# Cross attention and mixture of experts over 64 batches: the last part with fused small steps, a 65/12 split of the keys and new queue orders

## The chip, the cores and the metric

The kernel runs on one core of one Trainium2 chip. The metric is the device time of one execution in microseconds, taken over several runs. Profiles come from one further execution under the hardware profiler. TensorE does the matrix products, VectorE and ScalarE the elementwise work and reductions, GpSimd small side steps, and SyncE starts the transfers.

## What is computed

The reference is four layers, each an attention and a feed-forward part, on x of shape (64, 128, 128), with a context of 77 keys for each batch. Only the fourth layer's code changes. Cut to what matters, for each batch, with features the layer norm of x:

```python
txt_proj = textual_features @ Ws                      # 77 x 128
feat_proj = features @ W                              # 128 x 128
h = tanh(txt_proj[None, :, :] + feat_proj[:, None, :] + b)   # 128 tokens x 77 keys x 128
rho = h @ w + mask                                    # 128 x 77
att = softmax(rho)
txt_h = att @ textual_features
w_s, b_s = tanh(txt_h @ Wcw + bcw), tanh(txt_h @ Wcb + bcb)  # one number per token each
x = x + w_s * features + b_s
# then a mixture of 8 experts, routed to one, with a capacity, on xt = layer norm of x
probs = softmax(xt @ wg)
mask = one_hot(argmax(probs)) * (place in the expert's queue < capacity)
x = x + sum(probs * mask) * (W[expert] @ xt + b[expert])
```

## The kernel before

`part_3` (lines 2030 to 2378) is the last of the parts and runs the fourth layer batch by batch. Each engine has one queue. The order of its steps is written out by hand in the strings `ACT_D`, `DVE_D`, `PE_D` and `POOL_D` (lines 187 to 202): a word such as `x3.y@3` means that in turn p the engine does step x3.y of batch p - 3. `Order` (line 66) spells it out for 64 batches, and `go_through` (line 89) takes one step after another from the generators of each chain. Every step ends with an increment of its engine's semaphore, and a reader waits for that step's place in the order. So a turn is one pass through the string, and up to six batches are under way at once.

Attention, chain x3. VectorE takes the statistics of x (`bn_stats`, `bn_aggr`, lines 2289 and 2292), GpSimd makes the reciprocal root (lines 2114, 2117), VectorE normalises into xn (line 2295). TensorE transposes it (x3.T, line 2198) and makes the two projections (x3.proj, lines 2202 to 2205), ScalarE copies them out (lines 2128, 2135, 2136). For four chunks of 16 keys VectorE forms the sum of key and feature columns (x3.sum0 to x3.sum3, line 2310) in one of four buffers th, ScalarE takes the tanh (t0 to t3, line 2160), and TensorE multiplies by w (r.rho0 to r.rho3, line 2214). The last 13 keys, the tail, need no sum: ScalarE takes the tanh with the key's column as bias (ta with 7 keys, tb with 6, line 2171), and TensorE does r.rhoL. In r.rho a key is a product with 32 weight columns, and four keys go to four column strips of the array. ScalarE copies rho (x3.rho, line 2141), TensorE transposes it and adds the mask (r.rhoT, lines 2232, 2233), VectorE takes the largest (x3.nmax, line 2314), ScalarE the exponential with its sum (x3.exp, line 2146), TensorE transposes the result to 77 rows (p.PT, line 2241) and, after a copy (x3.PT, line 2150), makes the two gate columns (p.gate, line 2244). VectorE scales these (x3.rden, x3.gb, lines 2317, 2321), ScalarE takes their tanh (x3.gate, line 2153), and VectorE applies them: x3.y (line 2324) forms xn * w_s + b_s, and x3.x (line 2327) adds it to x.

Experts, chain f3. A norm as above into xf, a transpose (f3.T, line 2252, copied at line 2180), the router product of 8 columns (f3.route, line 2255). Then VectorE: largest logit (f3.nmax, line 2338), ScalarE: f3.exp (line 2183), VectorE: largest exponential (f3.emax, line 2341), reciprocal of the sum (f3.rden, line 2343), equal to the largest (f3.eq, line 2346), the first of those (f3.first, f3.pick, lines 2349, 2352), the running count (f3.taken, line 2359). TensorE places the tokens (f3.place, lines 2259, 2260), VectorE keeps those below the capacity (f3.keep, line 2363), TensorE transposes that (f3.kT, line 2263, copied at line 2186) and spreads it over 8 experts with products of 24 rows (f3.g, line 2269). VectorE multiplies tokens with it (f3.xm, line 2370), TensorE does the expert product (f3.y, lines 2273, 2275), VectorE forms the gate (f3.gate, line 2367) and adds the result to x (f3.out, line 2375). SyncE stores that batch (line 2102) and loads another (lines 2093, 2094).

Of the kernel before, what the change touches and what calls it, by code (L numbers as in the profile page):

```python
# [34 lines left out]
KEYS = 77  # L35
# [96 lines left out]
def take_turns(steps, chains):  # L132
# [52 lines left out]
    x1.rstd@3 f2.eps@8 f2.rstd@8 f1.eps@4 f1.rstd@4 x2.eps@6 x2.rstd@6 in.gather x1.eps@2  # L185
"""
ACT_D = """
    f3.kT@5 tb.tanh@1 x3.PT@3 t1.tanh@1 x3.rho@2 t0.tanh@1 x3.gate@3 x3.xT f3.xT@4 ta.tanh@1 f3.exp@4 x3.proj
    t2.tanh@1 x3.exp@2 t3.tanh@1
"""  # L190
DVE_D = """
    f3.pick@5 f3.taken@5 x3.sum0@1 f3.keep@5 f3.gate@5 x3.stats x3.sum1@1 x3.aggr f3.xm@5 x3.sum2@1 x3.norm x3.rden@3
    f3.norm@4 x3.gb@3 f3.out@5 x3.sum3@1 f3.nmax@4 x3.y@3 x3.nmax@2 x3.x@3 f3.stats@3 f3.emax@4 f3.rden@4 f3.eq@4
    f3.first@4 f3.aggr@3
"""
PE_D = """
    r.rho2@2 f3.kT@5 p.PT@3 f3.g@5 r.rho3@2 p.gate@3 f3.y@5 x3.T r.rhoT@2 f3.T@4 x3.proj f3.route@4 r.rho0@1 r.rhoL@1
    r.rho1@1 f3.place@4
"""
POOL_D = """  # L200
    f3.rstd@4 x3.eps x3.rstd f3.eps@3
"""
# [1827 lines left out]
def part_3(nc, d, shared):  # L2030
# [4 lines left out]
    ROWS = 32  # L2035
    CHUNKS = 4
    TAIL = KEYS - CHUNKS * KT
    KPAD = (CHUNKS + 1) * KT
    WIDE = 4 * ROWS
    FEAT = KEYS  # L2040
    with ExitStack() as ctx:
# [18 lines left out]
        cg = ring(NX, "cg3", [KEYS, 2])  # L2060
        th = ring(NT, "th3", [128, KT, TOK])
        tl = ring(2, "tl3", [128, TAIL, TOK])
# [61 lines left out]
        def _(act):  # L2124
            def x3(e):
# [28 lines left out]
                yield  # L2154

            def chunk(c):
                def chain(e):
                    act.wait_ge(dve_done, DVE_L.value(f"x3.sum{c}", e))
                    b = th[(CHUNKS * e + c) % NT]
                    nc.scalar.activation(b[:], b[:], ACT.Tanh).then_inc(act_done, ACT_L.did(f"t{c}.tanh", e))  # L2160
                    yield
                return chain

            def tail(p, keys):
                def chain(e):
                    s, r = e % NX, e % 2
                    act.wait_ge(act_done, ACT_L.value("x3.proj", e))
                    if e >= 2:
                        act.wait_ge(pe_done, PE_L.value("r.rhoL", e - 2))
                    for k in keys:  # L2170
                        last = nc.scalar.activation(tl[r][:, k, :], tf[s][:, FEAT:FEAT + TOK], ACT.Tanh, bias=tf[s][:, CHUNKS * KT + k:CHUNKS * KT + k + 1])  # L2171
                    last.then_inc(act_done, ACT_L.did(f"{p}.tanh", e))
                    yield
                return chain
# [13 lines left out]

            go_through(ACT_L, dict(x3=x3, t0=chunk(0), t1=chunk(1), t2=chunk(2), t3=chunk(3), ta=tail("ta", range(0, 7)), tb=tail("tb", range(7, TAIL)), f3=f3))

        @block.tensor
        def _(pe):
# [90 lines left out]
        def _(dve):  # L2283
# [14 lines left out]
            def x3(e):  # L2298
# [126 lines left out]
```

## Time and profile before

| | |
|---|---|
| median of 3 runs | 3166.46 us (3161.79 to 3166.59) |
| profiled execution | 3171.38 us, span 3169.5 us |
| PE busy over the span | 2764.2 us, 87% |
| DVE busy over the span | 2665.0 us, 84% |
| ACT busy over the span | 2449.1 us, 77% |
| POOL busy over the span | 895.2 us, 28% |

PE is TensorE (PEld its weight loads), DVE VectorE, ACT ScalarE, POOL GpSimd. Matrix products overlap each other and their ends are modelled, so a busy PE is not PE at its peak. Shares over the whole span mix several parts with different limits; the last part runs from about 2241 us to the end. The granted clock is that of TensorE, as a share of 2.4 GHz.

### The profile page before, as it was taken

What the parts mean: (1) busy time and instruction counts of PE and PEld (TensorE: products, weight loads), DVE (VectorE), ACT (ScalarE), POOL (GpSimd) and SP (SyncE); (2) the same over time, 40 slices, a digit from 0 to 9 for tenths busy, and PEclk for the clock granted to TensorE, in tenths of its full rate; (3) what the DMA queues carried; (4) which work ended last, traced back from release to release, by engine and by line L of the source; (5) the groups of instructions that cost most, each with busy time, mean ns of one, the idle gap of its engine ahead of it and who ended that gap; (6) DMA issues with size and microseconds to landing.
All of it is one profiled execution on the core that took longest, in us unless ns stands there. A gap on an engine that the chain in (4) does not pass through costs nothing. (4 is left out here: it accounts for less than half of the span.)

```text
span 3169.5 us, 77929 instructions
## 1 busy us (share of the span) xinstructions
PE 2764.2 (87%) x28057; PEld 1988.6 (63%) x28057; DVE 2665.0 (84%) x7187; ACT 2449.1 (77%) x6169; POOL 895.2 (28%) x1693
## 2 busy tenths in 40 slices
PE   6999999999999679979999997877588888888887
PEld 4666666666666446656767764325467776766765
DVE  4999999999999436469999995787699999999996
ACT  3888888888889435547777772787599899999995
POOL 1333333333333200045555540000122222222221
PEclk7999999999999689989999997998799889999998
DMA  1012121111111021101111111001100000000000
GB/s 48 26 33 60 50 36 33 34 33 33 33 33 32 13 62 43 41 21 34 35 34 35 33 29 28 1 0 50 53 13 15 13 15 15 15 14 14 15 15 9
DMA packets 177629, 91.13 MB, mean 29 GB/s; under 512 B 46339, under 2 KB 174021, under 8 KB 177251
## 3 DMA queue, kind: packets, MB, share of 16 engines
q1 hardware_dynamic: 171716, 76.85, 9.0%
q0 software_dynamic: 4096, 8.40, 0.8%
q8 instruction: 231, 3.78, 0.5%
q14 instruction: 146, 1.20, 0.1%
q10 hardware_dynamic: 1440, 0.90, 0.1%
HBM read 43.73 MB, written 42.36 MB: 27 GB/s over the span
## 5 line engine op out<-in xcount | busy, mean ns | idle before, releaser
L2310 DVE TENSOR_TENSOR th<-tf 128x2048 f32<-128x2048 f32 x256 | 583.5, 2279 | 10.3 <-PE p_rho L2214 6.4
L2160 ACT ACTIVATE th<-th 128x2048 f32<-128x2048 f32 x256 | 488.8, 1910 | 5.3 <-DVE th L2310 5.3
L653 ACT ACTIVATE probf<-probf,colf 128x128 f32<-128x128 f32 x1024 | 312.2, 390 | 0.0
L2214 PE MATMUL p_rho<-th,late_w_row 128*32 128x128 f32 x8192 | 299.5, 284 | 13.1 <-ACT th L2160 13.1
L2171 ACT ACTIVATE tl<-tf 128x128 f32<-128x128 f32 x832 | 256.8, 389 | 0.1
L2214 PEld LDWEIGHTS p_rho<-th,late_w_row 128*32 128x32 f32 x8192 | 227.8, 112 | 27.5 <-ACT th L2160 17.9
L1766 PE MATMUL acc<-xnT_all,wT 128*128 128x512 f32 x384 | 181.3, 625 | 29.6 <-DVE tmax L1958 13.2
L2275 PE MATMUL p_f<-w_pair,xm 128*128 128x128 f32 x1024 | 167.1, 330 | 0.0
L627 ACT COPY probT<-xp 77x1024 f32<-77x1024 f32 x128 | 129.1, 1009 | 48.6 <-PE xp L748 48.6
L953 DVE TENSOR_TENSOR probf<-fs,causal 128x1024 f32<-128x1024 f32 x128 | 155.2, 1212 | 8.1 <-PE fs L789 8.1
L1766 PEld LDWEIGHTS acc<-xnT_all,wT 128*128 128x128 f32 x384 | 73.5, 198 | 135.0 <-issue 83.0
L2114 POOL TENSOR_SCALAR col<-col 128x1 f32<-128x1 f32 x64 | 22.0, 344 | 479.9 <-DVE col L2292 479.9
L2275 PEld LDWEIGHTS p_f<-w_pair,xm 128*128 128x128 f32 x1024 | 153.3, 237 | 5.2
L2114 POOL TENSOR_SCALAR colf<-colf 128x1 f32<-128x1 f32 x64 | 15.6, 244 | 497.8 <-DVE colf L2292 497.8
L956 DVE TENSOR_REDUCE colf<-probf 128x8 f32<-128x1024 f32 x128 | 154.7, 1209 | 0.1
L1188 POOL TENSOR_TENSOR col<-col,minus_half 128x1 f32<-128x1 f32 x256 | 146.4, 572 | 21.3
L789 PE MATMUL fs<-kblkf,qTf 32*128 32x512 f32 x512 | 147.8, 654 | 3.0 <-POOL kblkf L562 2.3
L1442 DVE SCALAR_TENSOR_TENSOR hb<-tb,p_gv 128x512 f32<-128x512 f32 x67 | 46.0, 687 | 122.3 <-ACT tb L1212 90.4
L2117 POOL TENSOR_TENSOR colf<-colf,minus_half 128x1 f32<-128x1 f32 x64 | 146.3, 2286 | 5.3
L801 PE MATMUL fp<-ident,probf 128*128 128x128 f32 x1024 | 141.5, 283 | 4.1 <-ACT xncT L598 2.4
L748 PE MATMUL xp<-ident,prob 128*77 128x128 f32 x1024 | 141.2, 282 | 2.3 <-ACT prob L618 1.5
L623 ACT ACTIVATE prob<-prob,col 128x77 f32<-128x77 f32 x512 | 134.6, 348 | 6.6 <-DVE col L901 6.6
(434 smaller groups left out, 8171.6 us busy)
## 6 DMA issues: line engine op xcount, KB each, us to landing
rows<-zeros SPq DMA_DIRECT2D x64, 256.0 KB, 2.4
cxT<-in_ctxT SPq DMA_DIRECT2D x128, 38.5 KB, 2.0
xb<-rows SPq DMA_DIRECT2D x67, 64.0 KB, 1.8
rows<-yb SPq DMA_DIRECT2D x67, 64.0 KB, 1.5
x<-in_x SPq DMA_DIRECT2D x64, 64.0 KB, 1.8
x_mid<-x SPq DMA_DIRECT2D x64, 64.0 KB, 1.5
z<-x_mid SPq DMA_DIRECT2D x64, 64.0 KB
x_next<-z SPq DMA_DIRECT2D x64, 64.0 KB, 1.5
```

What stands on the lines that cost most here:

```text
L653: last = nc.scalar.activation(scores, scores, ACT.Exp, bias=colf[s][:, 16 + HALF * hf + h:17 + HALF * hf + h])
L789: last = nc.tensor.matmul(fs[:, b, :], qTf[s][g0:g0 + GROUP * HDIM, :], kblkf[s][g0:g0 + GROUP * HDIM, :, :], start=True, stop=True, tile_ ...
L953: nc.vector.tensor_tensor(scores, fs[:].rearrange("p b (h k) -> p (b h) k", h=GROUP), causal[:].unsqueeze(1).to_broadcast([128, HALF, TOK] ...
L956: nc.vector.tensor_reduce(colf[s][:, 16 + HALF * hf:16 + HALF * (hf + 1)], scores, X_AXIS, ALU.max, negate=True).then_inc(dve_done, DVE_L. ...
L1188: nc.gpsimd.tensor_tensor(col[s][:, 9:10], col[s][:, 8:9], minus_half[:], ALU.pow).then_inc(pool_done, POOL_M.did(f"{p}.rstd", e))
L1766: last = nc.tensor.matmul(acc[n][:, k, :], wT[:, m, k * CH:(k + 1) * CH], xnT_all[:, i * TTILE:(i + 1) * TTILE], start=True, stop=True)
L2117: nc.gpsimd.tensor_tensor(c[:, 9:10], c[:, 8:9], minus_half[:, 0:1], ALU.pow).then_inc(pool_done, POOL_L.did(f"{p}.rstd", e))
L2160: nc.scalar.activation(b[:], b[:], ACT.Tanh).then_inc(act_done, ACT_L.did(f"t{c}.tanh", e))
L2171: last = nc.scalar.activation(tl[r][:, k, :], tf[s][:, FEAT:FEAT + TOK], ACT.Tanh, bias=tf[s][:, CHUNKS * KT + k:CHUNKS * KT + k + 1])
L2214: last = nc.tensor.matmul(p_rho[r][ROWS * b:ROWS * (b + 1), 0:TOK], w_row[:, ROWS - 1 - a:2 * ROWS - 1 - a], tanh[:, k, :], start=(a == 0) ...
L2275: last = nc.tensor.matmul(p_f[:, 256:256 + DIM], xm[r][:, n, :], w_exp[:, n, :], start=False, stop=(n == MOE3 - 1))
L2310: nc.vector.tensor_tensor(th[i % NT][:], tf[s][:, n * KT:(n + 1) * KT].unsqueeze(2).to_broadcast([128, KT, TOK]), tf[s][:, FEAT:FEAT + TOK ...
```

## The change

In the last part:
- The chunks have 16, 16, 16 and 17 keys, and the tail has 12 (6 in ta and 6 in tb). `th` gets room for 17 keys.
- x3.y is gone. x3.x is one instruction, xn * w_s + x. The addition of b_s to x is a step x3.shift on ScalarE, which waits for f3.norm of the same batch: the norm of the expert part takes its input without b_s, which is one number for each token and so has no part in the norm. f3.out waits for x3.shift.
- f3.emax and f3.gate are gone. f3.eq compares with 1.0, and f3.out multiplies by the reciprocal of the sum.
- The four orders are new.

```diff
 PE_D = """
+    f3.kT@5 f3.g@5 p.gate@3 r.rho2@2 f3.y@5 r.rho3@2 f3.T@4 f3.route@4 x3.T r.rhoT@2 r.rho0@1 x3.proj p.PT@2
+    f3.place@4 r.rhoL@1 r.rho1@1
-    r.rho2@2 f3.kT@5 p.PT@3 f3.g@5 r.rho3@2 p.gate@3 f3.y@5 x3.T r.rhoT@2 f3.T@4 x3.proj f3.route@4 r.rho0@1 r.rhoL@1
-    r.rho1@1 f3.place@4
 ACT_D = """
-    f3.kT@5 tb.tanh@1 x3.PT@3 t1.tanh@1 x3.rho@2 t0.tanh@1 x3.gate@3 x3.xT f3.xT@4 ta.tanh@1 f3.exp@4 x3.proj
-    t2.tanh@1 x3.exp@2 t3.tanh@1
+    f3.exp@4 x3.xT x3.exp@2 tb.tanh@1 x3.proj x3.PT@2 t2.tanh@1 f3.kT@4 t3.tanh@1 t0.tanh ta.tanh x3.gate@2 x3.shift@3
+    x3.rho@1 f3.xT@3 t1.tanh
 DVE_D = """
-    f3.pick@5 f3.taken@5 x3.sum0@1 f3.keep@5 f3.gate@5 x3.stats x3.sum1@1 x3.aggr f3.xm@5 x3.sum2@1 x3.norm x3.rden@3
-    f3.norm@4 x3.gb@3 f3.out@5 x3.sum3@1 f3.nmax@4 x3.y@3 x3.nmax@2 x3.x@3 f3.stats@3 f3.emax@4 f3.rden@4 f3.eq@4
-    f3.first@4 f3.aggr@3
+    x3.sum2@2 f3.nmax@5 x3.x@4 x3.nmax@3 f3.rden@5 f3.eq@5 f3.stats@4 f3.first@5 x3.rden@3 f3.aggr@4 f3.pick@5
+    f3.taken@5 x3.sum3@2 f3.keep@5 x3.sum0@1 f3.xm@5 x3.stats x3.gb@3 x3.aggr x3.sum1@1 f3.out@5 x3.norm f3.norm@4
 POOL_D = """
-    f3.rstd@4 x3.eps x3.rstd f3.eps@3
+    f3.eps@4 f3.rstd@4 x3.eps x3.rstd
@@ part_3
-    CHUNKS = 4
-    TAIL = KEYS - CHUNKS * KT
-    KPAD = (CHUNKS + 1) * KT
+    CHUNK = (0, KT, 2 * KT, 3 * KT, 4 * KT + 1)
+    CHUNKS = len(CHUNK) - 1
+    TAIL = KEYS - CHUNK[-1]
+    KPAD = 80
...
+                act.wait_ge(act_done, ACT_L.value("x3.gate", e))
+                act.wait_ge(dve_done, DVE_L.value("f3.norm", e))
+                nc.scalar.activation(x[e % NR][:], x[e % NR][:], ACT.Identity, bias=col[s][:, 23:24]).then_inc(act_done, ACT_L.did("x3.shift", e))
+                yield
...
                 if e >= NX:
-                    after("x3.y", e - NX)
+                    after("x3.x", e - NX)
...
-                nc.vector.tensor_scalar(xn[s][:], xn[s][:], c[:, 22:23], c[:, 23:24], ALU.mult, ALU.add).then_inc(dve_done, DVE_L.did("x3.y", e))
-                yield
-                after("x3.y", e)
-                nc.vector.tensor_tensor(x[q][:], x[q][:], xn[s][:], ALU.add).then_inc(dve_done, DVE_L.did("x3.x", e))
+                nc.vector.scalar_tensor_tensor(x[q][:], xn[s][:], c[:, 22:23], x[q][:], ALU.mult, ALU.add).then_inc(dve_done, DVE_L.did("x3.x", e))
...
-                nc.vector.tensor_reduce(c[:, 19:20], c[:, 24:32], X_AXIS, ALU.max).then_inc(dve_done, DVE_L.did("f3.emax", e))
-                yield
...
-                after("f3.emax", e)
-                nc.vector.scalar_tensor_tensor(c[:, 32:40], c[:, 24:32], c[:, 19:20], first[:], ALU.is_equal, ALU.mult).then_inc(dve_done, DVE_L.did("f3.eq", e))
+                nc.vector.scalar_tensor_tensor(c[:, 32:40], c[:, 24:32], 1.0, first[:], ALU.is_ge, ALU.mult).then_inc(dve_done, DVE_L.did("f3.eq", e))
...
-                after("f3.rden", e)
-                nc.vector.tensor_tensor(c[:, 21:22], c[:, 18:19], c[:, 19:20], ALU.mult).then_inc(dve_done, DVE_L.did("f3.gate", e))
-                yield
...
-                after("f3.gate", e)
+                after("f3.rden", e)
                 dve.wait_ge(pe_done, PE_L.value("f3.y", e))
-                nc.vector.scalar_tensor_tensor(x[q][:], p_f[:, 256:256 + DIM], c[:, 21:22], x[q][:], ALU.mult, ALU.add).then_inc(dve_done, DVE_L.did("f3.out", e))
+                dve.wait_ge(act_done, ACT_L.value("x3.shift", e))
+                nc.vector.scalar_tensor_tensor(x[q][:], p_f[:, 256:256 + DIM], c[:, 18:19], x[q][:], ALU.mult, ALU.add).then_inc(dve_done, DVE_L.did("f3.out", e))
```

## Rows read from the trace of the kernel before

**Rows 1.** Busy time by stretch: the steady middle (PE, PEld, DVE, ACT, POOL, then clock).

```profile
2306.70:3118.10 811.40, 697.48 (x11745) 567.99 (x11741) 780.14 (x1535) 761.74 (x1712) 202.60 (x236) 0.92 0.06 15
```

**Rows 2.** VectorE in order of time, f3.xm only (start us, duration us).

```profile
2306.71 1.19 DVE L2370 TENSOR_TENSOR xm<-p_g,xfT 128x1024 f32<-128x1024 f32 x1
...
2694.70 1.19 DVE L2370 TENSOR_TENSOR xm<-p_g,xfT 128x1024 f32<-128x1024 f32 x1
...
2710.02 1.19 DVE L2370 TENSOR_TENSOR xm<-p_g,xfT 128x1024 f32<-128x1024 f32 x1
...
2723.24 1.19 DVE L2370 TENSOR_TENSOR xm<-p_g,xfT 128x1024 f32<-128x1024 f32 x1
...
3118.06 1.21 DVE L2370 TENSOR_TENSOR xm<-p_g,xfT 128x1024 f32<-128x1024 f32 x1
```

**Rows 3.** TensorE in order of time, ahead of a clock fall, and one turn later.

```profile
2692.43 0.33 PE L2241 MATMUL p_p<-ident,prob 128*77 128x128 f32 x1
2693.25 0.62 PE L2269 MATMUL p_g<-keptT,late_pick_row 24*128 24x128 bf16 x8 [0.48 <-ACT keptT L2186]
2693.80 1.08 PE L2214 MATMUL p_rho<-th,late_w_row 128*32 128x128 f32 x32
2695.16 0.38 PE L2244 MATMUL p_p<-cg,probT 77*128 77x2 f32 x2 [0.28 <-ACT probT L2150]
2695.94 0.28 PE L2273 MATMUL p_f<-late_b_bf,keptT 24*128 24x128 bf16 x1 [0.40 <-DVE xm L2370]
2696.15 3.78 PE L2275 MATMUL p_f<-w_pair,xm 128*128 128x128 f32 x16
...
2711.42 2.05 PE L2275 MATMUL p_f<-w_pair,xm 128*128 128x128 f32 x16
```

**Rows 4.** Busy time by stretch at the fall; the clock is the third number from the end.

```profile
2695.00:2695.50 0.50, 0.34 (x2) 0.30 (x2) 0.50 (x1) 0.50 (x2) 0.42 (x2) 1.00 0.04 16
2695.50:2696.00 0.50, 0.10 (x2) 0.06 (x1) 0.50 (x2) 0.50 (x1) 0.24 (x1) 0.50 0.00 0
```

**Rows 5.** VectorE in order of time, the small steps of a 13.22 us turn.

```profile
2716.56 0.34 DVE L2324 TENSOR_SCALAR xn<-xn,col 128x128 f32<-128x128 f32 x1
2716.82 0.28 DVE L2314 TENSOR_REDUCE col<-p_rT 128x1 f32<-128x128 f32 x1
2717.02 0.28 DVE L2327 TENSOR_TENSOR x<-x,xn 128x128 f32<-128x128 f32 x1
2717.33 0.29 DVE L2289 BATCH_NORM_STATS2 colf<-x 128x6 f32<-128x128 f32 x1
2717.54 0.15 DVE L2341 TENSOR_REDUCE colf<-colf 128x1 f32<-128x8 f32 x1
2717.60 0.16 DVE L2343 RECIPROCAL colf<-colf 128x1 f32<-128x1 f32 x1
2717.72 0.23 DVE L2346 SCALAR_TENSOR_TENSOR colf<-colf,first 128x8 f32<-128x8 f32 x1
2717.98 0.16 DVE L2349 TENSOR_REDUCE colf<-colf 128x1 f32<-128x8 f32 x1
```

**Rows 6.** ScalarE in order of time, from one kT copy to the next.

```profile
2708.36 0.26 ACT L2186 COPY keptT<-p_f 24x128 bf16<-24x128 bf16 x1 [0.39 <-PE p_f L2263]
...
2714.85 0.27 ACT L2180 COPY xfT<-p_f 128x128 f32<-128x128 f32 x1 [0.31 <-PE p_f L2252]
2715.01 2.15 ACT L2171 ACTIVATE tl<-tf 128x128 f32<-128x128 f32 x7
2717.07 0.25 ACT L2183 ACTIVATE colf<-p_f,colf 128x8 f32<-128x8 f32 x1
...
2721.49 0.24 ACT L2186 COPY keptT<-p_f 24x128 bf16<-24x128 bf16 x1
```

**Rows 7.** Groups by line and form, last part, the chunks' sum and tanh.

```profile
L2310 DVE TENSOR_TENSOR th<-tf 128x2048 f32<-128x2048 f32 x256 | 583.5, 2279 | 10.3 <-PE p_rho L2214 6.4 <-ACT cg L2136 3.2 <-issue 0.5
L2160 ACT ACTIVATE th<-th 128x2048 f32<-128x2048 f32 x256 | 488.8, 1910 | 5.3 <-DVE th L2310 5.3
```

More of the change, by code:

```diff
@@ L186 @@
 """
+PE_D = """
+    f3.kT@5 f3.g@5 p.gate@3 r.rho2@2 f3.y@5 r.rho3@2 f3.T@4 f3.route@4 x3.T r.rhoT@2 r.rho0@1 x3.proj p.PT@2
+    f3.place@4 r.rhoL@1 r.rho1@1
+"""
 ACT_D = """
-    f3.kT@5 tb.tanh@1 x3.PT@3 t1.tanh@1 x3.rho@2 t0.tanh@1 x3.gate@3 x3.xT f3.xT@4 ta.tanh@1 f3.exp@4 x3.proj
-    t2.tanh@1 x3.exp@2 t3.tanh@1
+    f3.exp@4 x3.xT x3.exp@2 tb.tanh@1 x3.proj x3.PT@2 t2.tanh@1 f3.kT@4 t3.tanh@1 t0.tanh ta.tanh x3.gate@2 x3.shift@3
+    x3.rho@1 f3.xT@3 t1.tanh
 """
 DVE_D = """
-    f3.pick@5 f3.taken@5 x3.sum0@1 f3.keep@5 f3.gate@5 x3.stats x3.sum1@1 x3.aggr f3.xm@5 x3.sum2@1 x3.norm x3.rden@3
-    f3.norm@4 x3.gb@3 f3.out@5 x3.sum3@1 f3.nmax@4 x3.y@3 x3.nmax@2 x3.x@3 f3.stats@3 f3.emax@4 f3.rden@4 f3.eq@4
-    f3.first@4 f3.aggr@3
-"""
-PE_D = """
-    r.rho2@2 f3.kT@5 p.PT@3 f3.g@5 r.rho3@2 p.gate@3 f3.y@5 x3.T r.rhoT@2 f3.T@4 x3.proj f3.route@4 r.rho0@1 r.rhoL@1
-    r.rho1@1 f3.place@4
+    x3.sum2@2 f3.nmax@5 x3.x@4 x3.nmax@3 f3.rden@5 f3.eq@5 f3.stats@4 f3.first@5 x3.rden@3 f3.aggr@4 f3.pick@5
+    f3.taken@5 x3.sum3@2 f3.keep@5 x3.sum0@1 f3.xm@5 x3.stats x3.gb@3 x3.aggr x3.sum1@1 f3.out@5 x3.norm f3.norm@4
 """
 POOL_D = """
-    f3.rstd@4 x3.eps x3.rstd f3.eps@3
+    f3.eps@4 f3.rstd@4 x3.eps x3.rstd
 """
@@ L2060, in part_3 @@
         cg = ring(NX, "cg3", [KEYS, 2])
-        th = ring(NT, "th3", [128, KT, TOK])
+        th = ring(NT, "th3", [128, KT + 1, TOK])
         tl = ring(2, "tl3", [128, TAIL, TOK])
@@ L2158, in chain @@
                     act.wait_ge(dve_done, DVE_L.value(f"x3.sum{c}", e))
-                    b = th[(CHUNKS * e + c) % NT]
-                    nc.scalar.activation(b[:], b[:], ACT.Tanh).then_inc(act_done, ACT_L.did(f"t{c}.tanh", e))
+                    b = th[(CHUNKS * e + c) % NT][:, 0:CHUNK[c + 1] - CHUNK[c], :]
+                    nc.scalar.activation(b, b, ACT.Tanh).then_inc(act_done, ACT_L.did(f"t{c}.tanh", e))
                     yield
@@ L2170, in chain @@
                     for k in keys:
-                        last = nc.scalar.activation(tl[r][:, k, :], tf[s][:, FEAT:FEAT + TOK], ACT.Tanh, bias=tf[s][:, CHUNKS * KT + k:CHUNKS * KT + k + 1])
+                        last = nc.scalar.activation(tl[r][:, k, :], tf[s][:, FEAT:FEAT + TOK], ACT.Tanh, bias=tf[s][:, CHUNK[-1] + k:CHUNK[-1] + k + 1])
                     last.then_inc(act_done, ACT_L.did(f"{p}.tanh", e))
@@ L2187, in f3 @@
                 yield
-            go_through(ACT_L, dict(x3=x3, t0=chunk(0), t1=chunk(1), t2=chunk(2), t3=chunk(3), ta=tail("ta", range(0, 7)), tb=tail("tb", range(7, TAIL)), f3=f3))
+            go_through(ACT_L, dict(x3=x3, t0=chunk(0), t1=chunk(1), t2=chunk(2), t3=chunk(3), ta=tail("ta", range(0, TAIL // 2)), tb=tail("tb", range(TAIL // 2, TAIL)), f3=f3))
         @block.tensor
@@ L2214, in add @@
                         last = nc.tensor.matmul(p_rho[r][ROWS * b:ROWS * (b + 1), 0:TOK], w_row[:, ROWS - 1 - a:2 * ROWS - 1 - a], tanh[:, k, :],
-                                                start=(a == 0), stop=(a == CHUNKS * KT // 4 - 1), tile_position=(0, ROWS * b))
+                                                start=(a == 0), stop=(CHUNK[-1] - 4 <= first_key + k < CHUNK[-1]), tile_position=(0, ROWS * b))
                     return last
@@ L2221, in rho @@
                         pe.wait_ge(act_done, ACT_L.value("x3.rho", e - 2))
-                    add(c * KT, th[(CHUNKS * e + c) % NT], KT).then_inc(pe_done, PE_L.did(f"r.rho{c}", e))
+                    add(CHUNK[c], th[(CHUNKS * e + c) % NT], CHUNK[c + 1] - CHUNK[c]).then_inc(pe_done, PE_L.did(f"r.rho{c}", e))
                     yield
@@ L2226, in rho @@
                         pe.wait_ge(act_done, ACT_L.value("tb.tanh", e))
-                        add(CHUNKS * KT, tl[r], TAIL).then_inc(pe_done, PE_L.did("r.rhoL", e))
+                        add(CHUNK[-1], tl[r], TAIL).then_inc(pe_done, PE_L.did("r.rhoL", e))
                         yield
@@ L2309, in x3 @@
                         dve.wait_ge(pe_done, PE_L.value(f"r.rho{(i - NT) % CHUNKS}", (i - NT) // CHUNKS))
-                    nc.vector.tensor_tensor(th[i % NT][:], tf[s][:, n * KT:(n + 1) * KT].unsqueeze(2).to_broadcast([128, KT, TOK]),
-                                            tf[s][:, FEAT:FEAT + TOK].unsqueeze(1).to_broadcast([128, KT, TOK]), ALU.add).then_inc(dve_done, DVE_L.did(f"x3.sum{n}", e))
+                    shape = [128, CHUNK[n + 1] - CHUNK[n], TOK]
+                    nc.vector.tensor_tensor(th[i % NT][:, 0:shape[1], :], tf[s][:, CHUNK[n]:CHUNK[n + 1]].unsqueeze(2).to_broadcast(shape),
+                                            tf[s][:, FEAT:FEAT + TOK].unsqueeze(1).to_broadcast(shape), ALU.add).then_inc(dve_done, DVE_L.did(f"x3.sum{n}", e))
                     yield
```

## The prediction

> **What bounds the kernel now.** I read four views in this order. The table by stretch [rows 1] sets the frame: only the last part changes, and its steady middle takes 811.4 us. VectorE is busy for 780.1 of them, ScalarE for 761.7, and the mean granted clock of TensorE is 0.92.
>
> The order of time on VectorE then gives the turn, the repeat of all steps for one batch. There is one xm step in a turn, 64 in all, and its starts mark the turns [rows 2]. From 2306.71 to 3118.06 lie 59 turns (the last four xm steps come later), 13.75 us each on average. But there are two kinds: 13.22 (2710.02 to 2723.24) and up to 15.32 (2694.70 to 2710.02). In the 13.22 kind VectorE goes from step to step with no wait. 59 turns of 13.22 are 780.0, so 31.4 us are lost in the longer ones.
>
> The order of time on TensorE shows why they are longer [rows 3]: the sixteen records of the expert products take 2.05 us in one turn and 3.78 in another. The granted clock goes from 1.00 to 0.50, the lower of its two levels (1.2 GHz), at 2695.5 [rows 4]. That is 0.8 us after an xm step began. I went through the steady middle in windows of half a microsecond: 19 falls, of which 17 lie 0.57 to 1.56 us after an xm start. So one place in the turn loses the clock. What TensorE did ahead of it [rows 3]: a transpose that gives 77 rows, a wait of 0.48, eight products of 24 rows, the 32 small-column records of rho3 (full, since four run side by side), a wait, two records of two columns, a wait of 0.40. The next large work is the expert product. At half clock TensorE can't do a turn in 13.22 and VectorE waits for it.
>
> So two things bound the stage: VectorE's queue of steps at full clock, and the clock falls on top.
>
> **The change part by part.** All durations are of the profiled execution (3171.38 us, span 3169.5). It is 4.9 above the median of the runs, 3166.46; I take the gain off the median.
>
> *VectorE's turn* [rows 5, 7]. Steps cost the distance to the next start. Removed: y, 0.26; emax, 0.06; f3.gate, a step of one column, taken as emax, 0.06; and the wait of the x step behind y and of first behind eq. The latter is 0.26 from eq to first, where an independent step (nmax behind y at 0.26, emax at 0.06) shows that a step of this size needs some 0.15: 0.11, because f3.stats now stands between them. The x step becomes one with three operands; its bounds are 0.20 (nmax, same size, one operand) and 0.31 (x now, with its wait). I take 0.26, as y, a gain of 0.05. Rden to eq, 0.12 now, has the emax wait in it; 0.04 goes. Added: one key more in sum3, 2.279/16 = 0.14. Sum: 13.22 - 0.26 - 0.06 - 0.06 - 0.11 - 0.05 - 0.04 + 0.14 = **12.78**.
>
> *ScalarE's turn* [rows 6, 7]. From one kT copy to the next lie 13.13 us (2708.36 to 2721.49), 0.31 of them idle ahead of the xfT copy; the 0.39 ahead of the first kT copy lies outside. Own work 12.82. Added: one key in t3, 1.910/16 = 0.12, and an Identity with a bias column on 128x128, x3.shift. No row of this stage shows that one; the nearest is a tail tanh of the same form, seven in 2.06 us, 0.29 each. Bounds: 0.16 (a plain copy of that size, xfT to the tail behind it) and 0.39 (a tail tanh from start to end, 2.15 less six times 0.29). Removed: one tail key, 0.29. Sum: **12.94**. Rows say that the add is no cheaper on ScalarE (0.29) than the y step was on VectorE (0.26). The Trainium skill, ScalarE: Activation LUTs, section Rules for kernel authors, says to give adds and multiplies to VectorE and not to ScalarE. By that rule the shift alone would be a loss; the sum stays as above.
>
> *Where the two meet.* Both queues are now full, so a round trip between them can be longer than either. I laid the new orders out by hand with these distances, in us from the start of sum2. VectorE: nmax 2.20, f3.rden 2.7, sum3 3.6, f3.keep 6.0, sum0 6.1, xm 8.3, sum1 9.8, f3.out 12.0, f3.norm 12.5. ScalarE, beside it: f3.exp 2.4, tb 3.2, t2 5.35, kT 7.2, t3 7.3, t0 9.2, ta 11.0, x3.shift 12.9, t1 13.5. TensorE: kT 6.7, g 7.5, gate 8.1, rho2 8.4, expert product 9.5, rho3 11.6, f3.T 12.9.
> The round trip: from f3.exp's start to its sum 0.35 (0.25 in [rows 6] and some 0.1 for the read of the sum, an estimate); hand-over 0.05 (an estimate, half of the overlap of two steps); VectorE from f3.rden to the end of f3.norm, 12.78 less sum2 (2.28 - 0.08 overlap = 2.20), less nmax, x and x3.nmax (0.06 + 0.26 + 0.20), less f3.norm's distance (0.26, as y), plus its full 0.34: 10.14. Hand-over 0.05. Then ScalarE's x3.shift 0.29, rho and xfT copies 0.16 each, t1.tanh 1.91 - 0.10 = 1.81, together 2.42, and f3.exp again. Sum **13.0** a turn. Behind x3.shift's new wait (for f3.norm of the same batch) stand the rho copy, the xfT copy and t1.tanh; TensorE waits for all of them, but in the layout that I made from the rows none of its steps is later than its reader: g (ends 8.1) lands 0.15 us ahead of xm, the expert product (ends 11.6) 0.4 ahead of f3.out. The first is the tightest. GpSimd's two steps for a norm lie well ahead of their readers in both orders; no DMA is added or moved, the store still follows f3.out.
>
> *Clock.* In the new order kT, g and gate no longer stand beside the 77-row transpose, which moves behind x3.proj with place; and rho2 comes right behind gate, with the expert product behind it. The stretch up to the expert product that holds only one full block of 16 keys was 3.7 us long at least (2692.43 to 2696.15, [rows 3]); in my layout it is 2.8 (kT 6.7 to 9.5), and elsewhere the waits stand between full products. I therefore take the steady falls as gone: -31.4. Bounds: nothing gained (falls as now), and the other side in the rival below.
>
> *Sum.* 59 x 13.00 = 767.0 against 811.4: **-44.4**. In the drain, behind 3118.1, the f3 steps run as one serial chain; f3.norm now stands behind f3.out there, 0.34 a turn more, against about 0.1 from emax: +1 over four turns. The fill has the same steps; 0, give or take 3. x3.x instead of x3.y as the step that frees a buffer costs nothing: it is long past. Net -43.4; 3166.5 - 43.4 = **3123 us**.
>
> **Rivals.**
> *A: the falls stay, only the turn gets shorter.* The falls could depend on something other than these products' size. The rows for this: TensorE's waits there are all short, 0.48 at most in [rows 3], it is busy 86% of the time in [rows 1] (697.5/811.4), and its clock falls all the same. Against: 17 of 19 at one place of the turn. The time: -13.0 (59 x 0.22) +1, 3154; where half the falls stay, 3139. The Trainium skill, TensorE: Matmul & The Clock Gate, section HAM oscillation, has the clock lost through long idle gaps between bursts, and not through the size of the products. By that rule no fall would occur at all in this stage, and shuffling product sizes would change none. The trace disagrees with the first half already [rows 3, 4].
> *B: the clock holds, the turn doesn't shorten.* g is 0.15 ahead of xm in my layout, and one late hand-over (kT copy behind t2.tanh on ScalarE, then g, then xm) eats the 0.22. The time: 59 x 13.22, -31.4 + 1: 3136.
> *C: slower.* The clock now falls in every turn, because the turn's phase no longer drifts past the weak place as it did, and 15.3 us becomes the rule. Place: the stretch from kT to the expert product, which waits for xm. Price: 2.1 us for a turn at the lower level (15.32 - 13.22); it decides from more than 21 of the 59 turns (44.4/2.1), where now the loss amounts to 15 (31.4/2.1). All turns: 59 x 15.1 = 891, +80, 3247. For it: TensorE waits for xm and for kT in the new order as well. Against: rho2 now fills that stretch.
> *D: both better than said*: x3.shift hides, no round trip binds, 12.80 a turn, and the fill gains 3: 3166.5 - 56.2 - 3 + 1, 3108.
>
> **How the numbers follow.** Forecast with D as its edge 0.66; A 0.16; B 0.12; C 0.05, and 0.01 for a turn that is lengthened by falls to about what it was. This kernel's runs can tell apart 0.2%, 6.3 us. The forecast, D, B and most of A lie below 3160: faster 0.93, with 0.01 of A's chance and that 0.01 given to the same, 0.02. C is slower, 0.05. The range goes from D with the bounds of x3.shift (-3), 3105, to A, 3154; what it leaves out is C and the worse half of A.
>
> **What would show it.** Right: the xm starts stand 12.9 to 13.1 apart through the middle; mean clock there 0.98 or more, no fall between 2400 and 3050; VectorE's wait sits ahead of f3.rden or f3.eq (released by f3.exp), ScalarE's ahead of x3.shift (by f3.norm); x3.shift near 390 ns. Wrong: falls at a fixed place of the new turn (A, C); xm waiting for g in every turn (B); a turn of 12.8 (D); or x3.shift far over 400 ns.

## The result, and the profile after

The changed kernel takes 3155.97 us (median of 8 runs, 3149.99 to 3162.43); the kernel before, in the runs taken beside these, 3168.65. The ratio is 0.9962, with a 95% interval of 0.9949 to 0.9975: faster, by 12 us and not by 43. The forecast of 3123 us and its range up to 3154 missed it.

Busy time by stretch, changed kernel: the steady middle from the first to the sixtieth f3.xm, and the one stretch in it at the lower clock (columns as in [rows 1]).

```profile
2297.30:3098.10 800.80, 634.37 (x11744) 517.52 (x11743) 759.18 (x1357) 762.47 (x1712) 458.40 (x236) 1.00 0.06 15
2719.20:2722.60 3.40, 3.40 (x16) 3.28 (x16) 2.29 (x3) 2.85 (x8) 2.75 (x2) 0.50 0.00 0
```

Against [rows 1] the middle is shorter by 10.6 us only (811.4 to 800.8), though the granted clock went from 0.92 to 1.00 and VectorE has 21 us less to do (780.1 to 759.2). The third number that moved is GpSimd's: 202.6 busy us became 458.4, for the same 236 steps.

VectorE in order of time, changed kernel, a whole turn but for some small steps (start us, duration us):

```profile
2502.08 0.18 DVE L2297 BATCH_NORM_AGGREGATE col<-col 128x2 f32<-128x6 f32 x1
2502.18 2.27 DVE L2316 TENSOR_TENSOR th<-tf 128x2048 f32<-128x2048 f32 x1
2504.37 0.34 DVE L2373 SCALAR_TENSOR_TENSOR x<-p_f,colf,x 128x128 f32<-128x128 f32 x1
2505.22 0.34 DVE L2300 TENSOR_SCALAR xn<-x,col 128x128 f32<-128x128 f32 x1 [0.51 <-POOL col L2117]
2505.48 0.34 DVE L2300 TENSOR_SCALAR xf<-x,colf 128x128 f32<-128x128 f32 x1
...
2508.27 0.28 DVE L2320 TENSOR_REDUCE col<-p_rT 128x1 f32<-128x128 f32 x1
2508.72 0.16 DVE L2344 RECIPROCAL colf<-colf 128x1 f32<-128x1 f32 x1 [0.17 <-ACT colf L2188]
...
2515.62 0.18 DVE L2297 BATCH_NORM_AGGREGATE col<-col 128x2 f32<-128x6 f32 x1
```

From x3.aggr to x3.aggr it is 13.54 us, against 13.22 in the quick turns of [rows 2]. The new wait stands ahead of x3.norm: 0.51 idle, released by GpSimd. A smaller one, ahead of f3.rden, is the hand-over from f3.exp. 56 of the 59 turns lie between 13.54 and 13.62, and only one (14.43) holds a clock fall, 1.56 us after its f3.xm began. Two others are 13.82 and 13.77.

GpSimd in order of time, changed kernel, in the same turn, and ScalarE at x3.shift and at the next f3.exp:

```profile
2502.35 2.18 POOL L2114 TENSOR_SCALAR col<-col 128x1 f32<-128x1 f32 x1 [1.21 <-DVE col L2297]
2504.61 0.57 POOL L2117 TENSOR_TENSOR col<-col,minus_half 128x1 f32<-128x1 f32 x1
...
2505.91 0.40 ACT L2158 ACTIVATE x<-x,col 128x128 f32<-128x128 f32 x1 [0.63 <-DVE xf L2300]
...
2508.34 0.27 ACT L2188 ACTIVATE colf<-p_f,colf 128x8 f32<-128x8 f32 x1
```

x3.eps, an addition on one column, takes 2.18 us. It starts 0.17 after the chunk's sum on VectorE (2502.18) and ends 0.08 after it (2504.53 against 2504.45). It stood still while the sum ran. Groups by line and form over the middle, GpSimd, first the kernel before:

```profile
L2117 POOL TENSOR_TENSOR colf<-colf,minus_half 128x1 f32<-128x1 f32 x59 | 141.5, 2399 | 4.9
L2117 POOL TENSOR_TENSOR col<-col,minus_half 128x1 f32<-128x1 f32 x59 | 33.5, 568 | 4.9
L2114 POOL TENSOR_SCALAR col<-col 128x1 f32<-128x1 f32 x59 | 13.1, 223 | 142.4 <-DVE col L2292 142.4
```

and the changed kernel:

```profile
L2114 POOL TENSOR_SCALAR colf<-colf 128x1 f32<-128x1 f32 x59 | 145.7, 2470 | 258.1 <-DVE colf L2297 258.1
L2114 POOL TENSOR_SCALAR col<-col 128x1 f32<-128x1 f32 x59 | 126.8, 2150 | 75.4 <-DVE col L2297 75.4
```

The same step in the kernel before, GpSimd in order of time, one turn; the f3.xm beside it runs there from 2502.14 to 2503.33:

```profile
2502.32 0.22 POOL L2114 TENSOR_SCALAR col<-col 128x1 f32<-128x1 f32 x1 [2.75 <-DVE col L2292]
2502.62 0.57 POOL L2117 TENSOR_TENSOR col<-col,minus_half 128x1 f32<-128x1 f32 x1
```

Both steps begin and end inside f3.xm, so a long neighbour alone does not stop them.

The sign was there before: one instruction, the power on one column, took 568 ns in the x3 chain and 2399 in the f3 chain. In the old order x3.aggr stood right ahead of f3.xm, whose one input is in PSUM; in the new one it stands right ahead of sum1, which has two inputs in SBUF.

What each turn then costs: waits of 0.51 and 0.17, with the overlap of two steps that a wait also ends, make 0.59 and 0.25 between starts, and VectorE's own work is 13.54 - 0.84 = 12.70.

### The profile page after: what moved, and what is told of

It reads as the page before. It is cut to its first block and busy times, and to the rows that moved or that the text cites. A ratio compares the mean times of both kernels' runs of the same rounds, so it can differ in the third digit from the quotient of the medians.

```text
span 3154.8 us, 77801 instructions
## 1 busy us (share of the span) xinstructions
PE 2699.0 (86%) x28057; PEld 1936.6 (61%) x28057; DVE 2641.0 (84%) x6995; ACT 2450.1 (78%) x6169; POOL 1160.3 (37%) x1693
## 3 DMA queue, kind: packets, MB, share of 16 engines
q14 instruction: 145, 1.19, 0.1%
## 5 line engine op out<-in xcount | busy, mean ns | idle before, releaser
L2316 DVE TENSOR_TENSOR th<-tf 128x2048 f32<-128x2048 f32 (+1 forms) x256 | 591.9, 2314 | 3.6 <-ACT cg L2136 3.2
L2165 ACT ACTIVATE th<-th 128x2048 f32<-128x2048 f32 (+1 forms) x256 | 490.7, 1941 | 2.4 <-DVE th L2316 2.4
L2114 POOL TENSOR_SCALAR col<-col 128x1 f32<-128x1 f32 x64 | 135.8, 2121 | 398.6 <-DVE col L2297 398.5
L2114 POOL TENSOR_SCALAR colf<-colf 128x1 f32<-128x1 f32 x64 | 153.4, 2397 | 297.6 <-DVE colf L2297 297.6
L2176 ACT ACTIVATE tl<-tf 128x128 f32<-128x128 f32 x768 | 237.6, 399 | 0.0
L1765 PE MATMUL acc<-xnT_all,wT 128*128 128x512 f32 x384 | 176.3, 610 | 29.9 <-DVE tmax L1957 13.5
L542 POOL TENSOR_SCALAR col<-col 128x1 f32<-128x1 f32 x64 | 18.2, 284 | 401.0 <-DVE col L853 394.8
L1195 POOL DMA_INDIRECT ya<-rows,slots x64 | 68.4, 1069 | 253.9 <-DMA rows<-yb 243.8
L2117 POOL TENSOR_TENSOR colf<-colf,minus_half 128x1 f32<-128x1 f32 x64 | 157.6, 2462 | 5.3
L1184 POOL TENSOR_SCALAR col<-col 128x1 f32<-128x1 f32 x256 | 57.1, 223 | 270.2 <-DVE col L1473 192.0
```

The source lines that it names most:

```text
L1765: last = nc.tensor.matmul(acc[n][:, k, :], wT[:, m, k * CH:(k + 1) * CH], xnT_all[:, i * TTILE:(i + 1) * TTILE], start=True, stop=True)
L2114: nc.gpsimd.tensor_scalar(c[:, 8:9], c[:, 7:8], LN_EPS, None, ALU.add).then_inc(pool_done, POOL_L.did(f"{p}.eps", e))
L2117: nc.gpsimd.tensor_tensor(c[:, 9:10], c[:, 8:9], minus_half[:, 0:1], ALU.pow).then_inc(pool_done, POOL_L.did(f"{p}.rstd", e))
L2165: nc.scalar.activation(b, b, ACT.Tanh).then_inc(act_done, ACT_L.did(f"t{c}.tanh", e))
L2316: nc.vector.tensor_tensor(th[i % NT][:, 0:shape[1], :], tf[s][:, CHUNK[n]:CHUNK[n + 1]].unsqueeze(2).to_broadcast(shape), tf[s][:, FEAT:FE ...
```

## The experiments

In the table, "quick" is the turn without a clock fall, "falls" those in the 59 turns of the middle, "mean" the mean turn there. The first three columns are from the one profiled run, the ratio from timed runs against the kernel before on the same chip. The falls agree with the timed runs: the mean granted clock of the whole kernel is 0.951 or more in every run of the versions with at most three falls, and at most 0.948 in every run of the others except e10.

| kernel | quick | falls | mean | ratio (95%) |
|---|---|---|---|---|
| before | 13.22 | 19 | 13.75 | 1 |
| changed | 13.54 | 1 | 13.57 | 0.9962 (0.9949 to 0.9975) |
| e1 stats early | 13.12 | 20 | 13.66 | 0.9960 (0.9941 to 0.9979) |
| e4 norms swapped | 13.13 | 25 | 13.63 | 0.9965 (0.9950 to 0.9981) |
| e7 e1 padded | 13.52 | 3 | 13.62 | 0.9959 (0.9945 to 0.9973) |
| e5 e1 with products | 13.18 | 0 | 13.20 | 0.9891 (0.9868 to 0.9915) |
| e6 e5, norm first | 13.18 | 0 | 13.18 | 0.9882 (0.9861 to 0.9902) |
| e3 before, aggr late | 14.08 | 37 | 14.19 | 1.0107 (1.0078 to 1.0137) |
| e10 before padded | 13.54 | 16 | 13.88 | 1.0008 (0.9991 to 1.0025) |
| e2 before with products | 13.22 | 1 | 13.25 | 0.9909 (0.9878 to 0.9940) |
| e8 steps alone, old orders | 12.80 | 30 | 13.61 | 0.9981 (0.9964 to 0.9997) |
| e9 e8 with products | 12.80 | 0 | 12.81 | 0.9814 (0.9793 to 0.9834) |

**e3: put the GpSimd wait into the kernel before.**

```diff
-    ... x3.sum1@1 x3.aggr f3.xm@5 x3.sum2@1 x3.norm ...
+    ... x3.sum1@1 f3.xm@5 x3.aggr x3.sum2@1 x3.norm ...
```

> The kernel before with one swap on VectorE: x3.aggr behind f3.xm, so that x3.eps meets x3.sum2. GpSimd's order stays as before. Theory P: x3.eps goes from 0.22 to about 2.1 us, x3.norm waits about 0.5, and the 59 turns cost up to 59 x 0.5 = 30 us more, ratio about 1.009 (less where the longer turn has fewer clock falls). Theory Q: no change, x3.eps stays at 0.22, ratio 1.000.

Groups by line and form over the middle, GpSimd, and VectorE in order of time, both of e3:

```profile
L2114 POOL TENSOR_SCALAR col<-col 128x1 f32<-128x1 f32 x59 | 128.0, 2169 | 208.4 <-DVE col L2292 208.4
```

```profile
2732.21 0.17 DVE L2292 BATCH_NORM_AGGREGATE col<-col 128x2 f32<-128x6 f32 x1
2732.30 2.26 DVE L2310 TENSOR_TENSOR th<-tf 128x2048 f32<-128x2048 f32 x1
2735.33 0.35 DVE L2295 TENSOR_SCALAR xn<-x,col 128x128 f32<-128x128 f32 x1 [0.77 <-POOL col L2117]
```

One swap on VectorE, with GpSimd's order untouched, took x3.eps from 223 ns to 2169 and cost 1.07% of the whole. Theory P holds, and with a longer wait than expected (0.77): here f3.out does not stand between the sum and x3.norm. Theory Q falls. The longer turn did not save the clock: 21 of the 37 falls stand at the old place, 0.63 to 1.84 us after f3.xm began, and 16 at a new one, 6.3 to 7.3 us after it, behind a wait of 1.17 of TensorE for x3.norm.

**e1: take the wait out of the changed kernel.**

```diff
-    ... x3.sum3@2 f3.keep@5 x3.sum0@1 f3.xm@5 x3.stats x3.gb@3 x3.aggr x3.sum1@1 ...
+    ... x3.sum3@2 x3.stats f3.keep@5 x3.aggr x3.sum0@1 f3.xm@5 x3.gb@3 x3.sum1@1 ...
```

> The changed kernel with x3.stats and x3.aggr moved ahead of x3.sum0 on VectorE, nothing else. Theory P (port): GpSimd's small steps stand still while VectorE runs a step with two SBUF inputs (a sum of a chunk), and go on beside f3.xm, one of whose inputs is in PSUM. Then x3.eps falls in time beside f3.xm, takes 0.25 us instead of 2.12, VectorE's wait of 0.51 ahead of x3.norm is gone, and the turn goes from 13.54 to about 13.0: 59 x 0.54 = 32 us less than the changed kernel, near 3124. Theory Q (GpSimd's own queue: the new order of its steps, or dearer instructions): x3.eps stays at 2.1 us and the turn at 13.5, 3156.

The wait of x3.norm was gone and the quick turn went to 13.12, near the 13.0 of P. But x3.eps did not get shorter: it now stood still beside sum0, 1986 ns on average, and only ended well before its reader; so on x3.eps this run does not part P from Q; e3 does. And the time did not move: 0.9960. Busy time by stretch, e1, the middle:

```profile
2303.30:3109.50 806.20, 660.29 (x11741) 546.56 (x11733) 761.16 (x1356) 763.10 (x1712) 330.61 (x236) 0.96 0.06 15
```

The clock is back at 0.96. Twenty turns hold a fall, and such a turn takes 14.7. Every one of them begins 1.35 to 1.87 us after an f3.xm started. TensorE in order of time, e1, ahead of one, and busy time by stretch there:

```profile
2506.23 0.22 PE L2268 MATMUL p_f<-late_ident_bf,kept 128*24 128x128 bf16 x1
2506.92 0.61 PE L2274 MATMUL p_g<-keptT,late_pick_row 24*128 24x128 bf16 x8 [0.47 <-ACT keptT L2191]
2507.46 0.38 PE L2249 MATMUL p_p<-cg,probT 77*128 77x2 f32 x2
2507.78 1.08 PE L2219 MATMUL p_rho<-th,late_w_row 128*32 128x128 f32 x32
2509.37 0.22 PE L2278 MATMUL p_f<-late_b_bf,keptT 24*128 24x128 bf16 x1 [0.51 <-DVE xm L2367]
2509.52 3.41 PE L2280 MATMUL p_f<-w_pair,xm 128*128 128x128 f32 x16
```

```profile
2509.50:2510.00 0.50, 0.50 (x5) 0.48 (x5) 0.50 (x1) 0.50 (x1) 0.00 (x0) 0.96 0.00 0
2510.00:2510.50 0.50, 0.50 (x5) 0.50 (x4) 0.50 (x1) 0.50 (x2) 0.00 (x0) 0.50 0.00 0
```

So the new order still has a weak place: a transpose with 24 columns, a wait of 0.47, products of 24 rows, two of two columns, one full block, a wait of 0.51. The one fall of the changed kernel stands at the same place. By its number of falls this order is no better than the old one here (20 against 19); at turns of 13.5 it is (e7 and e10 below).

**e4: take f3.norm out of the wait instead.**

```diff
-    ... x3.sum1@1 f3.out@5 x3.norm f3.norm@4
+    ... x3.sum1@1 f3.out@5 f3.norm@4 x3.norm
```

> The changed kernel with f3.norm ahead of x3.norm on VectorE, nothing else. Theory R: the turn is set by the round trip f3.exp, f3.rden, f3.norm, x3.shift, t1.tanh, in which the wait of x3.norm for GpSimd stands only because it is ahead of f3.norm. Then f3.norm uses 0.26 of that wait, x3.shift starts 0.8 earlier, the bound becomes VectorE's own 12.70 plus a remaining wait of 0.33, a turn of about 13.0 and 30 us less than the changed kernel. Rival: ScalarE or TensorE binds anyway: the turn stays above 13.4.

The quick turn is 13.13, 0.1 above the expectation, and the waits ahead of f3.rden and x3.shift are gone, so the round trip over x3.shift did set the 13.54. The time is 0.9965, again with falls, 25 now, but at another place, 9.8 to 10.3 us after f3.xm began. TensorE in order of time, e4, the end of that stretch:

```profile
2515.45 0.45 PE L2207 MATMUL p_x<-cxT,late_w_txt 128*128 128x77 f32 x2 [0.38 <-ACT xnT L2128]
...
2516.41 0.31 PE L2246 MATMUL p_p<-ident,prob 128*77 128x128 f32 x1
2516.56 0.17 PE L2264 MATMUL p_f<-pick,late_before_bf 128*128 128x8 bf16 x1
2516.59 0.17 PE L2265 MATMUL p_f<-taken,late_ones_bf 128*128 128x8 bf16 x1
2517.66 0.86 PE L2219 MATMUL p_rho<-tl,late_w_row 128*32 128x128 f32 x24 [0.90 <-ACT tl L2176]
```

That the transpose p.PT and the placing, with a wait of 0.90 behind them, are the reason here was not tried by itself.

**e2: fill the weak place of the kernel before, with no order changed.**

```diff
 p.PT:   nc.tensor.transpose(p_p[0:KEYS, 0:TOK], ...)
+        nc.tensor.matmul(p_x[:, 336:464], w_feat[:], ident[:], start=True, stop=True)
 p.gate: nc.tensor.matmul(p_p[:, 128:130], ...)
+        nc.tensor.matmul(p_x[:, 336:464], w_feat[:], ident[:], start=True, stop=True)
```

> The kernel before, all orders as they were, with two added full products of 128 rows and 128 columns per turn whose result nobody reads: one behind p.PT and one behind p.gate, in TensorE's waits of about 0.48 and 0.40 us. Theory F1: the clock falls come from the stretch of products of few rows or columns; filled up, it no longer loses the clock: the falls go, the turn stays at 13.22, and the time goes down by about 31 us, ratio 0.990. Theory F2: the falls hang on the length of the turn or its phase, not on what is in that stretch: they stay, ratio 1.000 or a little above.

Busy time by stretch, e2, the middle:

```profile
2311.50:3093.30 781.80, 683.68 (x11981) 545.68 (x11977) 776.18 (x1534) 759.52 (x1712) 201.98 (x236) 1.00 0.06 15
```

Two useless products in each turn make the kernel before 0.91% faster. The middle went from 811.4 to 781.8, 29.6 less, against 31.4 worked out ahead from [rows 2]; one fall was left. The turn's length stayed, so what TensorE does in this stretch makes the falls. TensorE in order of time, e2, the stretch:

```profile
2508.03 0.34 PE L2241 MATMUL p_p<-ident,prob 128*77 128x128 f32 x1
2508.20 0.39 PE L2242 MATMUL p_x<-ident,late_w_feat 128*128 128x128 f32 x2
2508.84 0.62 PE L2271 MATMUL p_g<-keptT,late_pick_row 24*128 24x128 bf16 x8 [0.25 <-ACT keptT L2186]
...
2510.99 0.47 PE L2246 MATMUL p_x<-ident,late_w_feat 128*128 128x128 f32 x2
2511.54 0.23 PE L2275 MATMUL p_f<-late_b_bf,keptT 24*128 24x128 bf16 x1
```

The edit did two things at once: it put full products among the small ones, and it shortened the waits, from 0.48 to 0.25 and from 0.40 to none ([rows 3] has them before). It does not tell which of the two kept the clock, and no run here does. That waits alone are not enough is seen in e1: TensorE stands idle for 0.84 in every turn ahead of the tail's products, longer than anywhere in its weak place, and no fall stands there.

**e5: the same for e1.** One full product behind f3.kT, two behind r.rho2.

```diff
 f3.kT:   nc.tensor.transpose(p_f[0:3 * MOE3, 192:256]...)
+         nc.tensor.matmul(p_rT[:, 256:384], w_feat[:], ident[:], start=True, stop=True)
 r.rho2:  add(CHUNK[c], ...)
+         if c == 2: two times nc.tensor.matmul(p_x[:, 336:464], w_feat[:], ident[:], start=True, stop=True)
```

> e1_early_stats with three added full products per turn whose result nobody reads: one behind f3.kT (ahead of TensorE's wait for the kT copy) and two behind r.rho2 (ahead of its wait for f3.xm). Theory F1 (a stretch of products of few rows or columns with waits loses the clock, and e1 still has one, from f3.kT to the start of the expert product): the 20 falls, all 1.35 to 1.87 us after f3.xm began, go, the turn is 13.1 throughout, 59 x (13.66 - 13.12) = 32 us less than e1, ratio to the kernel before 0.986. Theory F2 (the length of the turn decides, not what stands in it): the falls stay, ratio 0.996.

No fall, and 0.9891, short of the 0.986 expected. The quick turn is 13.18, 0.06 above e1's: f3.out, which waits for the expert product, starts 2.38 after sum1 and not 2.32.

**e7: make e1's turn as long as the changed kernel's.**

```diff
+                if p == "x3":
+                    for b in pad:
+                        nc.vector.tensor_tensor(b[:], ident[:], ones[:], ALU.add)
                 dve.wait_ge(pool_done, POOL_L.value(f"{p}.rstd", e))
```

> e1_early_stats with two added VectorE steps of 128x128 ahead of x3.norm (0.20 us each, result unread), so that its turn is as long as that of the changed kernel, 13.5 us, with TensorE's order and products as they are. Theory F2 (the length of the turn decides in which turns the weak stretch costs the clock): the falls drop from 20 to a few, as in the changed kernel (1), and the time is within 0.2% of e1's in spite of 24 us of added work. Theory F1 alone (only the content of the stretch counts): about 20 falls stay and the time is 59 x 0.4 = 24 us above e1, ratio 1.003 to 1.005.

Three falls instead of twenty, at the same place (1.37 to 1.42 after f3.xm), and 0.9959 against 0.9960: 0.4 us of added work in every turn cost nothing. So F2 has a part as well: with TensorE's products and their order as they were, a turn longer by 0.4 took 17 of the 20 falls away. How the length does it is not shown.

**e10: make the turn of the kernel before as long.** The same edit with steps of 128x128 and 128x48.

> The kernel before, all orders as they were, with two added VectorE steps ahead of x3.norm (128x128 and 128x48, 0.32 us together, result unread), so that its turn is as long as that of the changed kernel, 13.54 us. It tells whether the changed kernel lost its falls through the new order of TensorE or through its longer turn. Theory O (order): the weak place of the old order still loses the clock, 15 or more falls, turn mean 14.0, ratio 1.005. Theory L (length of the turn): few falls, at most 5, the turn is 13.54 nearly throughout, and the time is no higher than before, ratio 0.996 to 1.000, in spite of 19 us of added work.

The falls are as O says, 16, and the time is nearly as L says, 1.0008 for 19 us of added work. In its first 32 turns there were two falls, then they came in a chain. The profiled run is the slowest of its ten (3190.23 us against a median of 3180.03), and the mean clock differs more among them (0.931 to 0.952) than in any other version, so the 16 is one draw of many. But nine of the ten lie below every run of the changed kernel (0.951 to 0.958) and of e7 (0.951 to 0.957). So at this length of turn the length alone does not explain the single fall of the changed kernel. The new order of TensorE is the likely part; the orders of the other engines and the chunk sizes differ as well, and were not parted from it.

**e8: the small steps alone, in the old orders.** The changed computation; the strings of before without x3.y, f3.emax and f3.gate, f3.stats behind f3.eq, and x3.shift@4 between x3.xT and f3.xT@4 on ScalarE.

> The changed kernel's computation (x3.y, f3.emax and f3.gate gone, x3.shift on ScalarE, 65 and 12 keys) in the old orders, with x3.shift put between x3.xT and f3.xT. The small steps alone: VectorE's own turn 12.7 to 12.8, ScalarE's 12.8, no x3.eps beside a chunk's sum (x3.aggr still stands ahead of f3.xm). If nothing else binds, the turn at full clock goes from 13.22 to 12.9 and the falls stay as before or grow more frequent: 19 us less for the turn, some 10 back for falls, ratio 0.997. Rival: the falls take all of it, ratio 1.000 or above.

A quick turn of 12.80, the shortest of all, for the wait for GpSimd does not exist in these orders. But 30 falls, with turns of 15.1 and 13.9, leave 0.9981. Fifteen stand at the old place (1.2 to 1.5 us after f3.xm began) and fifteen at 11.9 to 12.3; ahead of both TensorE waits 0.78 for the kT copy.

**e6: e5 with f3.norm ahead of f3.out and x3.norm.**

> e5_early_dummy with f3.norm ahead of f3.out and x3.norm on VectorE, so that the round trip over x3.shift is 0.5 us shorter. Theory R (the round trip sets the 13.12): the turn goes down to ScalarE's own work, 12.8 to 12.9, some 15 us less than e5, ratio 0.982. Rival: the turn stays at 13.1 because f3.out waits for the expert product or another hand-over takes its place.

0.9882, and still 13.18: the rival was right. x3.shift no longer waits. ScalarE now waits 0.17 for rho3 ahead of the rho copy, and VectorE 0.29 for f3.exp ahead of f3.rden. So another round trip, over rho3 and the rho copy, is as long as the one over x3.shift, and the 13.1 does not hang on x3.shift alone.

**e9: e8 with e2's two products.**

> e8_fused_old_order (the changed computation in the old orders, 12.8 us a turn at full clock, 30 falls) with the two added full products of e2, behind p.PT and behind p.gate. Theory F1: the falls go or nearly go, the turn is 12.8 throughout, 59 x (13.75 - 12.8) = 56 us less than before, ratio 0.982, faster than both kernels and than e6. Rival: the weak stretch is too weak for two products at this turn, or they delay the expert product and f3.out: some falls stay, ratio 0.988 to 0.995.

Busy time by stretch, e9, the middle:

```profile
2308.90:3064.40 755.50, 682.25 (x11973) 544.44 (x11965) 751.96 (x1357) 755.41 (x1710) 337.66 (x236) 1.00 0.06 16
```

No fall, 12.81 a turn, ratio 0.9814 (0.9793 to 0.9834): 3116.39 us against 3176.11 of the kernel before beside it. It beats both kernels and every other version here. ScalarE is busy for 755.4 of the 755.5 us and VectorE for 752.0, and in the turns looked at neither waits: both queues are full, and together they are the bound. f3.eps takes 2.30 us there, and VectorE does not wait for it.

## Why the prediction was wrong

*What bounds the kernel* held: a turn of 13.22, and falls at one place that cost 31. e2 gave back 29.6 of them.

*VectorE's own turn*: said 12.78, measured 12.70. *ScalarE's own*: said 12.94; 13.54 less the 0.72 between starts ahead of x3.shift gives 12.82. x3.shift takes 402 ns, against an upper bound of 390. These terms were right to about 0.1.

*Where the two meet*: said 13.0 for the round trip. Its parts in the changed kernel: f3.exp at 2508.34 to f3.rden at 2508.72, 0.38 (said 0.40); x3.shift at 2505.91 to the next f3.exp, 2.43 (said 2.42). With the GpSimd wait taken away (e1) the turn is 13.12. This was right to 0.1, and e4 shows that this trip set the 13.54. That nothing else would bind at 13.0 is not shown: in e6, with this trip shortened, the turn stays at 13.18.

**The step that failed** is one sentence: "GpSimd's two steps for a norm lie well ahead of their readers in both orders". It put the wait for GpSimd at nothing, with no row and no price for the two steps. At their old durations, 0.22 and 0.57, it would have held: the layout has sum1 at 9.8, right behind x3.aggr, and f3.out at 12.0. But beside a chunk's sum x3.eps takes 2.15, x3.norm waits 0.51, and the wait lies in the round trip. By e1, which takes it out, it costs 13.54 - 13.12 = 0.42 a turn, 59 x 0.42 = 25 us of the 34 by which the middle came out longer than forecast (800.8 against 767.0). Another 59 x 0.12 = 7 us are the round trip itself, 13.12 and not 13.00; the fall and the two odd turns are the rest. e3 makes the same wait in the kernel before with one swap. The Trainium skill says it in two places. GPSIMD Engine Reference, section Specifications, has GpSimd's SBUF interfaces shared with VectorE, with contention where a VectorE instruction has two SBUF inputs. SBUF — State Buffer, section Terms, says that the loser blocks for the full instruction. The trace agrees: 223 ns beside f3.xm, which reads PSUM and SBUF, 2150 to 2169 on average beside a sum of 2.27 us, from whose end on it needs only 0.08 more. None of my four rivals was about GpSimd.

**A second step would have failed behind it**: "I therefore take the steady falls as gone". They were gone in the result (0.98 or more was asked, 1.00 came), but partly thanks to the first error. At the turn of 13.12 that I had nearly forecast, the same order of TensorE has 20 falls and the same time (e1). So with the GpSimd wait avoided, the forecast would have missed as well, as rival A at 3154 had it. That rival carried 0.16. Its saving, 12 us, is nearly the measured one, but that is luck: the falls went, and the turn got longer. Its argument, that the size of the products might not matter, was not settled: e2 and e5 show that the stretch can be filled, and they change sizes and waits together. What I had not seen is that the new place is still weak, and that the length of the turn has a part in how often that shows. Rival B, the clock holds and the turn doesn't shorten, is the closest in shape, at 3136; but the hand-over that it named, g to xm, did not bind (VectorE waits 1.5 us in all ahead of f3.xm over the 59 turns), and the turn grew by 0.32 where B left it at 13.22. Rival C named the turn's length as a factor and gave it the wrong sign for this case. C and D did not happen.

The changed kernel gives 12 us: the middle's mean turn fell from 13.75 to 13.57, 59 x 0.18 = 10.6. With the falls gone by added products its computation, in the old orders, brings 59 us (e9). The fused steps are worth 0.42 a turn (13.22 to 12.80, e8), and the new orders gave that away again: 13.12 at best.

What stays open: why at one length of the turn nearly every third turn loses the clock and at another one in twenty to sixty; and what the two odd turns of 13.8 in the changed kernel are. In them VectorE stands still for 0.18 us ahead of sum3 and for 0.20 ahead of f3.stats, places where it does not wait in other turns, with no other engine releasing it; the one turn with a fall is the one right behind the first of them. Whether the short waits, the small products or both lose the clock is open too.

## What to carry to other kernels

When a small step is moved on one engine, look at what runs beside it on the engine that shares its memory port; here that is VectorE for GpSimd. An instruction with two typical durations in one profile (568 and 2399 ns here) is telling of such a neighbour; give a GpSimd step a partner on VectorE that has one input in PSUM, or let it end long before its reader.

Where the granted clock falls at one place of a repeated turn, try to fill TensorE's waits there with full products whose result is not used, before any order is rewritten: it cost two lines and gave 0.9% (e2), and 1.7% on top of e8. And do not read a gain in clock off one version: with the turn's length the number of falls moved, from 20 to 3 (e1 to e7), from 19 to 30 (e8) and to 37 (e3), though hardly in e10 (19 to 16). From e1 to e7 that hid 0.4 us in each turn, and in e8 most of a gain of 0.42.

## What the runs showed of the hardware

- An addition on 128x1 on GpSimd took 223 ns on average beside a VectorE step with one input in PSUM (f3.xm, 1.19 us), and 1986 to 2470 ns beside one with two inputs in SBUF. Beside the chunks' sums x3.eps ended 0.07 to 0.10 us after the sum did, in every turn of the changed kernel, e1 and e3 that has it.
- TensorE's granted clock fell from 1.00 to 0.50 though TensorE was never idle for long. In the 4 us ahead of a fall its longest wait was 0.45 to 0.55 us in the kernel before, about 0.5 in e1 (0.73 once), 0.78 in e8, 0.5 to 0.9 in e4, and 1.17 ahead of 16 of the 37 falls of e3. The stretches ahead of the falls in the kernel before, in e1 and in e4 held products with 24 or 77 rows, or 2 to 24 columns. Two added full products in each turn, which also shortened the waits, ended the falls (19 to 1 in e2, 30 to 0 from e8 to e9). The Trainium skill, TensorE: Matmul & The Clock Gate, section HAM oscillation, ties the loss of clock to long idle gaps; no such gap stands in these rows.
- Added VectorE work of 0.3 to 0.4 us in each of 64 turns left the time nearly as it was, twice (e7 beside e1; e10, whose interval ends at 1.0025, or 8 us for 19 us of added work).
